# Weighting the chosen experts' rows with one broadcast product on GpSimd in a vision tower block on Trainium2

## What is computed

```python
h = x @ tok_W + pe
h = h + attention(layernorm(h))                  # causal, 8 heads
flat = layernorm(layernorm(h)) * ln_scale + ln_bias
out_shared = swiglu(flat @ shared_in_w.T) @ shared_out_w.T + shared_out_b
g_idx = argmax(flat @ group_gate_w.T + group_bias)
e_probs = softmax(e_logits[g_idx] + expert_bias[g_idx])
topv, topi = top_k(e_probs, 2)
topv = topv / (topv.sum(-1, keepdims=True) + 1e-08)
h_expert = swiglu(flat @ expert_in_w.T)
comb[rows, g_idx * 4 + topi] += topv             # weight of each expert, 0 if not chosen
for e in range(8):
    routed = routed + comb[:, e:e + 1] * (h_expert @ expert_out_weight[e].T)
return h + out_shared + routed
```

## Time and profile before

| | |
|---|---|
| median of 3 runs | 1072.35 us (1069.49 to 1074.19) |
| the profiled execution's own time | 1073.58 us |
| its span, first to last instruction | 1071.9 us |
| PE busy (matmul) | 986.7 us, 92% |
| DVE busy | 777.3 us, 73% |
| ACT busy | 591.3 us, 55% |
| POOL busy | 322.1 us, 30% |
| mean granted TensorE clock | 0.984 |

### The profile page before, as it was taken

One profiled execution on the slowest core, in us unless ns is written; L12 is line 12 of the kernel. 1 busy time (PEld: TensorE's weight loads), 2 busy tenths in 40 slices (PEclk: granted clock), 3 DMA queues, 4 the chain that ended last, 5 costly groups with the idle time before them and its releaser, 6 DMA issues.

```text
span 1071.9 us, 17016 instructions
## 1 busy us (share of the span) xinstructions
PE 986.7 (92%) x5552; PEld 665.1 (62%) x5552; DVE 777.3 (73%) x2444; ACT 591.3 (55%) x1351; POOL 322.1 (30%) x466
## 2 busy tenths in 40 slices
PE   2598999999999999999999998999989999899976
PEld 2354556676657666676667666666657676575554
DVE  6478758885788857986688857987588858788233
ACT  2034655566554665557545765647655665446734
POOL 3031313324232223324142333323142242322334
PEclk9999999999999999999999999999999999899989
DMA  3540045003140045002350053100550041300000
GB/s 118 69 56 2 10 53 74 1 2 50 34 63 2 2 72 74 1 2 31 43 73 1 2 72 49 26 1 3 71 72 2 1 64 33 45 2 1 12 1 20
DMA packets 29480, 35.06 MB, mean 33 GB/s; under 512 B 5696, under 2 KB 15936, under 8 KB 29264
## 3 DMA queue, kind: packets, MB, share of 16 engines
q1 hardware_dynamic: 29392, 33.97, 21.5%
HBM read 4.02 MB, written 4.19 MB: 8 GB/s over the span
## 4 chain that ended last, share of the span: by engine, by line
PE 75%; DVE 9%; DMA 4%; ACT 3%; SPq 3%; issue 3%; POOL 2%; ACTq 0%; POOLq 0%; DVEq 0%
PE bank_p L580 14%; PE bank_s L553 13%; PE bank_w L598 11%; PE bank_f L679 5%; PE bank_f L680 5%; PE bank_f L681 5%; DMA q_stack<-qk_l 3%; PE bank_m L645 3%; PE bank_f L501 2%; SPq L449 2%; PE bank_f L503 2%; PE bank_f L502 2%; DVE mx_far L767 2%; PE bank_m L501 2%; ACT pt L1025 1%
## 5 line engine op out<-in xcount | busy, mean ns | idle before, releaser
L1025 ACT ACTIVATE pt<-bank_p 128x512 f32<-128x512 f32 (+3 forms) x768 | 350.0, 491 | 266.0 <-PE bank_p L580 260.6
L553 PE MATMUL bank_s<-k_stack,q_stack 112*128 112x512 f32 (+3 forms) x768 | 273.4, 394 | 36.3 <-DMA q_stack<-qk_l 12.5
L771 DVE CUSTOM_DVE_ANT_0 bank_s<-bank_s,causal 128x384 f32<-128x384 f32 (+3 forms) x512 | 246.0, 507 | 65.2 <-PE bank_s L553 60.7
L580 PE MATMUL bank_p<-q_stack,k_stack 128*128 128x512 f32 (+3 forms) x768 | 256.4, 379 | 5.3 <-ACT pt L1025 4.2
L553 PEld LDWEIGHTS bank_s<-k_stack,q_stack 112*128 112x128 f32 x768 | 146.9, 197 | 140.1 <-DVE mx L771 58.0
L767 DVE TENSOR_REDUCE mx_far<-bank_s 128x1 f32<-128x512 f32 x256 | 166.8, 684 | 35.2 <-PE bank_s L553 33.5
L1166 POOL TENSOR_SCALAR_AFFINE_SELECT pt<-pt 128x512 f32<-128x512 f32 x128 | 81.8, 639 | 361.0 <-ACT pt L1025 361.0
L580 PEld LDWEIGHTS bank_p<-q_stack,k_stack 128*128 128x128 f32 x768 | 138.9, 193 | 77.6 <-ACT pt L1025 48.7
L598 PE MATMUL bank_w<-pt,v 128*32 128x512 f32 (+3 forms) x1536 | 159.3, 497 | 0.6 <-POOL pt L1166 0.5
L679 PE MATMUL bank_f<-wex_h,hid_h 128*128 128x512 f32 x256 | 103.2, 403 | 0.1
L681 PE MATMUL bank_f<-wex_h,hid_l 128*128 128x512 f32 x256 | 101.2, 395 | 0.0
(11 more groups left out here) (130 smaller groups left out, 1351.5 us busy)
## 6 DMA issues: line engine op xcount, KB each, us to landing
q_stack<-qk_h SPq DMA_DIRECT2D x64, 128.0 KB, 3.9
k_stack<-qk_h SPq DMA_DIRECT2D x64, 128.0 KB, 5.8
q_stack<-qk_l SPq DMA_DIRECT2D x32, 128.0 KB, 5.2
k_stack<-qk_l SPq DMA_DIRECT2D x32, 128.0 KB, 5.9
out<-h SPq DMA_DIRECT2D x16, 256.0 KB, 4.3
x_sb<-x_t SPq DMA_DIRECT2D x16, 64.0 KB, 5.7
pt<-w_expert SPq DMA_DIRECT2D x1, 1024.0 KB, 5.6
pos_sb<-pos SPq DMA_DIRECT2D x2, 256.0 KB, 3.1
```

What stands on the lines that cost most here:

```text
L553: nc.tensor.matmul(s_bank[s % 2][:, 0:cols], q_stack[0:STACK, half, hd, t % HT * P:(t % HT + 1) * P], k_stack[0:STACK, hd // 2, key_place( ...
L580: nc.tensor.matmul(p_bank[p % 2][:, q0:HALF], k_stack[:, hd // 2, key_place(i, kt // HT), kt % HT * P:(kt % HT + 1) * P], q_stack[:, half, ...
L771: nc.vector.tensor_tensor_reduce(src, src, causal[:, HALF - cols:HALF], 1.0, -3.0e38, ALU.add, ALU.max, mx[:, u, col:col + 1]).then_inc(s_ ...
L1025: nc.scalar.activation(pt[:, k % PT_SLOTS, j, q0:HALF], p_bank[p % 2][:, q0:HALF], ACT.Exp, scale=0.25).then_inc(exp_done, 1)
```

## The change

The four multiplies on ACT go, and with them the semaphore `weighted` and ACT's part in the step "combine". POOL multiplies all four parts of `sel` in one instruction with `wsel`, whose four weights are broadcast over 128 columns each, in place. It waits for `sel_made` (DVE's sum) before, and for its own product before the first of the sums. COMBINE becomes 4, and the waits on `ex_step` count one step more. DVE's wait in the routing now goes by `ex_step`. The order of the steps on every engine stays as it was.

```diff
-COMBINE = 3
+COMBINE = 4
...
                 if part == 0:
                     if i:
-                        dve.wait_ge(weighted, ((i - 1) * TILES + (half + 1) * HT) * EG)
+                        dve.wait_ge(ex_step, ((i - 1) * TILES + (half + 1) * HT) * COMBINE)
...
-                elif kind == "combine":
-                    t = st[1]
-                    act.wait_ge(sel_made, i * TILES + t + 1)
-                    for e in range(EG):
-                        part = slice(e * P, (e + 1) * P)
-                        nc.scalar.mul(sel[:, t % 2, part], sel[:, t % 2, part],
-                                      wsel[:, t, e:e + 1]).then_inc(weighted, 1)
...
-                elif st[0] in ("in", "hid", "expert", "combine"):
+                elif st[0] in ("in", "hid", "expert"):
...
-                pool.wait_ge(weighted, (i * TILES + t + 1) * EG)
+                pool.wait_ge(sel_made, i * TILES + t + 1)
+                by_expert = four.rearrange("p (e c) -> p e c", e=EG)
+                nc.gpsimd.tensor_tensor(by_expert, by_expert, wsel[:, t, :].unsqueeze(2).to_broadcast([P, EG, P]),
+                                        ALU.mult).then_inc(ex_step, 1)
+                pool.wait_ge(ex_step, done + 1)
                 nc.gpsimd.tensor_tensor(two, four[:, 0:2 * P], four[:, 2 * P:4 * P], ALU.add).then_inc(ex_step, 1)
                 if t % HT == 0:
                     pool.wait_ge(m_taken, after(i, "shared", t // HT))
-                pool.wait_ge(ex_step, done + 1)
+                pool.wait_ge(ex_step, done + 2)
                 nc.gpsimd.tensor_tensor(mine, mine, two[:, 0:P], ALU.add).then_inc(ex_step, 1)
-                pool.wait_ge(ex_step, done + 2)
+                pool.wait_ge(ex_step, done + 3)
                 nc.gpsimd.tensor_tensor(mine, mine, two[:, P:2 * P], ALU.add).then_inc(ex_step, 1)
```

More of the change, by code:

```diff
@@ L383, in build @@
         hidh_made, hidl_made = sem("hidh_made"), sem("hidl_made")
-        ex_ready, sela_made, sel_made, weighted, ex_step = (
-            sem(n) for n in ("ex_ready", "sela_made", "sel_made", "weighted", "ex_step"))
+        ex_ready, sela_made, sel_made, ex_step = (sem(n) for n in ("ex_ready", "sela_made", "sel_made", "ex_step"))
         out_done = [sem(f"out_done_{n}") for n in range(H_SLOTS)]
```

## The result

The changed kernel took 1076.32 us (median of 12 runs, 1071.29 to 1077.10), beside 1071.19 us for the kernel before (12 runs): a ratio of 1.0037, 95% interval 1.0022 to 1.0052, so 4 us slower, in round numbers (2.4 to 5.6). The medians differ by 5.1 us, the means, by which the ratio goes, by 4.0. Measured a second time, unaltered, it took 1074.37 us (10 runs, 1072.06 to 1076.67) beside 1071.59: 1.0028 [1.0014, 1.0043], 3.0 us. Both intervals lie above 1 and they overlap; the two ratios average 1.0033, or 3.5 us. The forecast was 4.4 us more, 1077.

What follows compares the result with a forecast made beforehand. PE, busy 92% of the span, was taken as the bound. The terms 1.5 - 0.3 + 0.6 + 1.2 + 1.4 gave +4.4 us: 1078.0 for the profiled execution, 1077 for the median, range 1071 to 1085.

Steps and rivals of the forecast that it cites:

- the splits: Last image, middle: two splits of the hidden rows behind a combine end 1.34 us later, delaying PE's first expert matmul: +0.6 us.
- the port: Last image: the POOL product starts first and blocks DVE's two-input count L888, straight on the chain: +1.2 us, bounds 0 and 1.3.
- the tail: The last three combines stand end to end on POOL, without the cover of ACT's multiplies: +1.4 us.
- Price of the product: Each of 64 POOL products of 128x512 takes 1.28 us, bounds 0.74 and 2.58.
- Rival C: The product is dear, 2.4 us, making 1089, or 1083 at half the surcharge; chance 0.12.
- Steady masks: Images 1 to 6: a pt mask behind a longer combine starts 0.77 us later, delaying PE's weighting matmuls: +1.5 us in all.
- ACT relief: Steady images: PE's gate matmul L633 waits less for ACT work queued behind multiplies: -0.3 us, at most -1.7.
- Rival B: Most delays are swallowed, L888 gets the port first; the tail's 1.4 and the 0.6 are left, 1074.4; chance 0.27.
- Rival D: Products block DVE in more places than placed, ten blocks of 0.5 us on the chain, 1082; chance 0.13.
- Rival E: Faster: PE's waits for exponentials shrink as ACT's queue does, by 7.4 us; the tail's 1.4 stays, 1066.4; chance 0.08.

Runs made afterwards that it cites:

- no weights: The kernel before with the multiplies gone from ACT and not put on POOL, so the rows are not weighted at all: 1069.82 us, ratio 0.9987.
- product twice: The changed kernel with every POOL product done twice in place, so the weights are applied squared: 1085.60 us, ratio 1.0131.
- full operand: The changed kernel with a full 128x512 table added in place of the product with the broadcast weights: 1079.99 us, ratio 1.0070.
- twelve chosen tiles on ACT: The changed kernel with ACT multiplies kept for tiles ahead of masks, splits, count and in the tail, the other 52 on POOL: 1071.98 us, ratio 1.0007.
- the tail on ACT: The changed kernel with the last three tiles, (7,5) to (7,7), weighted by ACT multiplies as before: 1073.38 us, ratio 1.0020.

## Why the prediction was right, step by step

The direction and the places were right. The size came out right in part by luck: the splits, the port and the tail were put too high, and a fall of the clock that no step had made up for them. Start times of the same PE instruction in the second profile of the changed kernel, less those of before, in us, worked out from the two traces:

| at (time of before) | 240 | 365 | 900 | 990 | 1000 | 1046 | 1050 | 1056 | 1064 |
|---|---|---|---|---|---|---|---|---|---|
| later by | -1.64 | -2.65 | -1.49 | -1.95 | -1.57 | -1.71 | -0.92 | +0.30 | +0.30 |

- **Price of the product**: 1.28 us taken, 1.04 measured, within the bounds 0.74 to 2.58. It was put at the rows with the same elements and inputs, and the choice was wrong by 0.24 us: the product with an operand that stands still along the innermost dimension is cheaper for POOL, the sum with one broadcast over the middle dimension (L1151, 1279 ns) isn't. Rival C falls.
- **Steady masks, +1.5, and ACT relief, -0.3**: the differences between 240 and 900 also hold falls of the clock that only one kernel of a pair had, of about 0.9 us each (at 300.3 and at 546.1 of the kernel before). So the terms are read at single steps. In the same PE instructions against the kernel before, in us:

| profile | step at the late mask, images 1 to 6 | step at the gate matmul, images 0 to 5 |
|---|---|---|
| after, and again | +0.27 to +0.34 | -0.10 to -0.15 |
| no weights | 0.0 | -0.12 to -0.17 |
| product twice | +1.39 to +1.46 | |
| full operand | +0.52 to +0.57 | |
| twelve chosen tiles on ACT | 0.0 | 0.0 |

  The masks make six times 0.30, +1.8 us. The pause at L527 swallows the 0.3 each time, as the prediction had it for a part, but at the next L580 (L579) the 0.3 is there again: that matmul waits for the exponentials [the row of 498.84 above], which have moved too. ACT's relief comes where the prediction looked for it, at L633, and makes -0.8 us. Together it is +1.0, where the two terms made 1.2. Two pauses of 0.3 us at L552, which the profile puts down to the issue, come and go at 272 and 394 and cancel; the one at 394 is in the version without weights too.
- **Splits of the last image, +0.6**: 990 to 1000, +0.38, in both profiles of the changed kernel, 0.12 us of it from the mask ahead of them.
- **The port, +1.2**: 1046 to 1050, +0.79. The product was first, by 0.10 us, and L887 took 981 ns against 191. In every profile where a product stands there L887 ends about 0.05 us after it (1051.23 and 1051.18; 1048.80 and 1048.75; 1057.65 and 1057.60; with the full operand 1050.97 and 1050.93). This agrees with the rule of the Trainium skill (page "SBUF — State Buffer", section "Who interferes with whom") that of two such instructions the first one issued shuts the other out for its whole length. The term was mis-sized by the product's price and by 0.2 us in which L887 would have run anyway; and where the clock does not fall, the pause ahead of L679 takes 0.33 of the 0.79, so that 0.5 is left. Of the two stretched rows that the prediction named in support, only L894 has two inputs in SBUF; L884 has one.
- **The clock, not predicted**: 1050 to 1056, +1.22 more, in the second profile; from 1046 to 1056 it is 1.98 us in the first and 2.01 in the second, count and clock together. Against the 0.5 of the version with the tail on ACT, which has the wait without the fall, the fall costs about 1.5 us. It isn't in every execution.
- **The tail, +1.4**: +0.7. The reasoning, three combines end to end, was right, and the price was 2.87 and not 3.13 us each. By its own numbers, 1070.60 - 1069.12, the term was 1.5.

Measured terms: 1.0 + 0.4 + 0.5 + 0.7 = 2.6 us, and 1.0 + 0.4 + 2.0 + 0.7 = 4.1 where the clock falls; the two ratios give 4.0 and 3.0. How many of the executions had the fall is not known. Rival B's +2.0 us lies within the second interval; it falls by the traces, since the masks weren't swallowed and the count lost the port. Rival D falls: L887 is 191 to 196 ns in 15 of 16 places, the one other two-input line that is newly stretched, L860 at 981.5 (460 ns in place of 192), moves nothing on PE, and DVE's busy time rose by 0.3 us in all. Rival E falls by the list of waits and by the kernel with no weights.

The profiled execution of the first measurement shows 3.3 us more span than before's. Part of that is chance: the second profile of the same kernel has every PE start near 1020 2.8 us earlier than the first one. 1.4 us of this is there at 240 already: near 70 us a score matmul of 128x384 takes 0.52 us in the first and 0.33 in the second, which left the clock's lower level some 5 us sooner. The rest arises between 300 and 1034, where the falls of the clock differ from execution to execution. That is why the terms above are read across single steps and not from the sums.

## What to carry to other kernels

An engine's idle share says nothing on whether work may be put on its queue: look for what stands directly behind each new instruction, and for a short two-input instruction on VectorE's path that becomes ready just after a GpSimd instruction has started. Before moving work off an engine that mostly waits for the bound, take the work away entirely and time that; here that gave 1.4 us, under half of the 3.0 to 4.0 that the move lost. Where one product must lose against a short instruction on the chain, a wait on that one tile is cheap: here it cost 0.4 us of idle time, and by the traces it gave back 0.5 us, or 2 where the clock would have fallen.

## What the runs showed of the hardware

- GpSimd took 1042 ns for 128x512 with a second operand broadcast along the innermost dimension, 1271 to 1291 with a full one, and 1279 with one broadcast over the middle dimension. The first is a multiplication, the others are additions and a subtraction; the operation was not varied by itself.
- A VectorE operation of 191 ns with two SBUF inputs took 981 ns when it began 0.10 us behind such a product, and 1203 behind the longer one. It ended 0.04 to 0.05 us after GpSimd each time.
- A wait of TensorE of 1.23 to 1.45 us was followed in three executions of five by the granted clock at its lower level (1.2 GHz; 1051.3 to 1054.7 in the first profile), at which a 128x512 matmul took 0.63 us in place of 0.40; waits of 0.43 to 0.91 us in none of five. The fall cost about 1.5 us, more than the 0.8 by which the wait had been lengthened.
